# Identity attention's keys turned by transposes, their mean added behind them

## The reference

```
def _L0_tok_ref(x, W_h, b_h, W_o, b_o, W_r, b_r):     # patches of 16 samples and a mask
    hid = silu(einsum('bnd,dm->bnm', xm, W_h) + b_h)
    return einsum('bnm,mh->bnh', hid, W_o) + b_o + einsum('bnd,dh->bnh', xm, W_r) + b_r

def _L0_attn_ref(x):                                  # 16 heads of 16 columns
    xh = x.reshape(B, T, H, hd)
    x_centered = xh - mean(xh, axis=1)                # mean over the tokens
    corr = einsum('bthd,bThd->bhtT', x_centered, x_centered)
    return einsum('bhtT,bThd->bthd', softmax(corr, -1), xh)

h = _L0_tok_ref(x, ...)
h = h + _L0_attn_ref(_layernorm(h))
h = h + _L0_ffn_ref(_layernorm(h), ...)               # two layers, untouched here
```

## Time and profile before

| | us |
|---|---|
| median of 3 runs | 2703.74 |
| lowest and highest | 2702.42, 2705.84 |
| the profiled execution | 2703.38 |
| its span in the trace | 2701.6 |
| TensorE busy | 2600.9 (96% of the span) |
| VectorE busy | 1913.5 (71%) |
| ScalarE busy | 1702.6 (63%) |
| GpSimd busy | 1429.9 (53%) |

### The profile page before, as it was taken

The page is one execution under the profiler, slowest core; times in us unless marked ns, Lnnn a source line. Parts: engine busy times, 40 slices in busy tenths (PEclk is TensorE's granted clock), DMA queues, the critical chain, the costliest instruction groups (busy, mean ns, idle before and its releaser), DMA issues.

```text
span 2701.6 us, 71253 instructions
## 1 busy us (share of the span) xinstructions
PE 2600.9 (96%) x25088; PEld 2229.4 (83%) x25088; DVE 1913.5 (71%) x3771; ACT 1702.6 (63%) x4184; POOL 1429.9 (53%) x1520
## 2 busy tenths in 40 slices
PE   6999999969999999998999998999999998999998
PEld 4888888858888888877888887888888887888887
DVE  5777777658878788776656556887878877666664
ACT  3666666547778777774444435777777777444442
POOL 7888888557777776662000005777777665000000
PEclk9999999989999999998999999999999999999999
DMA  1111111111111111112111111111111111222221
GB/s 42 38 48 36 46 36 36 41 38 43 50 37 51 41 38 38 41 63 65 51 59 50 56 38 39 42 51 37 50 41 38 38 41 55 71 75 73 80 73 47
DMA packets 165614, 130.35 MB, mean 48 GB/s; under 512 B 23238, under 2 KB 163688, under 8 KB 165461
## 3 DMA queue, kind: packets, MB, share of 16 engines
q1 hardware_dynamic: 163157, 119.80, 14.3%
q0 software_dynamic: 2304, 8.47, 1.0%
HBM read 77.47 MB, written 50.33 MB: 47 GB/s over the span
## 4 chain that ended last, share of the span: by engine, by line
PE 48%; DVE 21%; ACT 20%; issue 7%; SPq 2%; DMA 1%; DVEq 1%; POOL 0%; ACTq 0%; POOLq 0%
ACT attn_E L1040 14%; PE const_banks L1317 6%; PE const_banks L1318 6%; PE const_banks L1319 6%; DVE attn_neg_top L1213 6%; DVE attn_ss L1206 5%; DVE attn_rot_b L1190 5%; ACT attn_sq L1077 5%; PE const_banks L1453 3%; PE const_banks L1452 3%; PE const_banks L1451 3%; PE const_banks L508 3%; PE const_banks L493 3%; PE const_banks L581 2%; PE const_banks L494 2%
## 5 line engine op out<-in xcount | busy, mean ns | idle before, releaser
L1040 ACT ACTIVATE attn_E<-const_banks,attn_nbias,attn_rn 128x128 f32<-128x128 f32 x1024 | 452.8, 462 | 144.9 <-DVE attn_nbias L1218 144.9
L977 POOL TENSOR_TENSOR attn_qk<-attn_rot_a,attn_rot_b 128x1024 f32<-128x1024 f32 x128 | 303.6, 2372 | 361.6 <-issue 296.2
L964 POOL TENSOR_TENSOR ffn_rstd<-ffn_var,const_neg_half 128x4 f32<-128x4 f32 x32 | 32.3, 1009 | 687.0 <-DVE ffn_var L1143 687.0
L1328 PE MATMUL const_banks<-weights_w_hi,attn_xT_hi 128*128 128x512 f32 x768 | 316.6, 412 | 1.2 <-DVE attn_oT_lo L1225 1.0
L1329 PE MATMUL const_banks<-weights_w_lo,attn_xT_hi 128*128 128x512 f32 x768 | 305.0, 397 | 0.0
L1330 PE MATMUL const_banks<-weights_w_hi,attn_xT_lo 128*128 128x512 f32 x768 | 304.8, 397 | 0.0
L1243 DVE SCALAR_TENSOR_TENSOR ffn_gated<-const_banks,weights_b_col,ffn_gate 128x512 f32<-128x512 f32 (+1 forms) x192 | 143.7, 749 | 216.3 <-ACT ffn_gate L1111 209.3
L1317 PE MATMUL const_banks<-ffn_xT_hi,ffn_w_hi 128*128 128x512 f32 x704 | 282.8, 402 | 6.9 <-DVE ffn_xT_lo L1155 5.4
L1318 PE MATMUL const_banks<-ffn_xT_lo,ffn_w_hi 128*128 128x512 f32 x704 | 279.5, 397 | 0.0
L1319 PE MATMUL const_banks<-ffn_xT_hi,ffn_w_lo 128*128 128x512 f32 x704 | 278.9, 396 | 0.0
L1111 ACT ACTIVATE ffn_gate<-const_banks,weights_b_col 128x512 f32<-128x512 f32 x160 | 110.1, 688 | 226.3 <-PE const_banks L1319 222.3
(11 more groups left out here) (178 smaller groups left out, 8009.9 us busy)
## 6 DMA issues: line engine op xcount, KB each, us to landing
attn_x_res<-xa SPq DMA_DIRECT2D x128, 128.0 KB, 4.9
xb<-attn_x_new SPq DMA_DIRECT2D x128, 128.0 KB, 1.7
ffn_x_<-xb SPq DMA_DIRECT2D x32, 512.0 KB
h<-ident_h SPq DMA_DIRECT2D x64, 128.0 KB, 1.7
xa<-ident_n SPq DMA_DIRECT2D x64, 128.0 KB, 1.7
attn_x_<-xa SPq DMA_DIRECT2D x128, 64.0 KB
xa<-ffn_x_new SPq DMA_DIRECT2D x16, 512.0 KB, 3.6
ffn_add<-h SPq DMA_DIRECT2D x16, 512.0 KB, 6.4
```

The costliest lines, as they stand in the source:

```text
L977: pool.tensor_tensor(qk[:, slot].rearrange("p a n -> p (a n)"), rot_a[:].rearrange("p a h d -> p (a h d)"), rot_b[:].rearrange("p a h d -> ...
L1040: last = act.activation(E[:, r, i], ps_s[:, r, i * P:(i + 1) * P], ACT.Exp, bias=nbias[:, r, i:i + 1], scale=rn[:, slot, h:h + 1], accum_o ...
L1328: pe.matmul(out_, xT_hi[:, slot, k], w.w_hi[:, k, cols], start=(k == 0), stop=False)
```

## The change

`centre` goes. The four matmuls of the keys become four transposes with the identity `c["ident"]`. VectorE sums the turned keys over the tokens, with the sign turned, into `nsum` (a new reduction between the two max reductions, which waits for the transposes). ScalarE's copy becomes four activations, one for each piece, that compute 128 v - sum, which is 128 times the centred value. The scores are then 128 x 128 times as large, and the exponential gets the scale 1/128^2. `cT_ready` is now counted up by the last of the four. On ScalarE the copy of the patches moves ahead of the keys' copy. GpSimd's preparation loses a memset and a select, and the counts of `cleared` and `pads` go down by one.

```diff
@@ front, GpSimd @@
-            for ap, value in ((centre[:], -1.0 / TOKENS), (sel[:], 0.0), (c["ident_b"][:], 0.0),
+            for ap, value in ((sel[:], 0.0), (c["ident_b"][:], 0.0),
                               (c["causal"][:], 0.0), (c["neg_half"][:], -0.5)):
                 pool.memset(ap, value).then_inc(cleared, 1)
-            pool.wait_ge(cleared, 6)
-            pool.affine_select(out=centre[:], in_=centre[:], compare_op=ALU.not_equal, fill=1.0 - 1.0 / TOKENS,
-                               base=0, pattern=[[-1, P]], channel_multiplier=1).then_inc(pads, 1)
+            pool.wait_ge(cleared, 5)
@@ ScalarE @@
-                if on(CENT):
-
-                    b = t - CENT
-                    need(act, s["cT_ps"], b + 1)
-                    need(act, s["S_ps"], b - 1)
-                    act.activation(cT[:, (u - CENT) % 2], ps_turn, ACT.Copy).then_inc(s["cT_ready"], 1)
                 if on(0) and u % 4 == 3:
...
                     act.activation(xT[:, u // 4], ps_hid[0:STACK], ACT.Copy).then_inc(xT_ready, 1)
+                if on(CENT):
+
+                    b = t - CENT
+                    need(act, s["summed"], b + 1)
+                    need(act, s["S_ps"], b - 1)
+                    for j in range(4):
+                        last = act.activation(cT[:, (u - CENT) % 2, j], ps_turn[:, j], ACT.Identity,
+                                              bias=nsum[:, (u - CENT) % 2, j:j + 1], scale=float(TOKENS))
+                    last.then_inc(s["cT_ready"], 1)
...
-                        act.activation(E[:, (u - SCORE) % 2, 2 * g:2 * g + 2], ps_S[:, 2 * g:2 * g + 2], ACT.Exp
-                                       ).then_inc(s["exp_done"], 1)
+                        act.activation(E[:, (u - SCORE) % 2, 2 * g:2 * g + 2], ps_S[:, 2 * g:2 * g + 2], ACT.Exp,
+                                       scale=1.0 / TOKENS ** 2).then_inc(s["exp_done"], 1)
@@ VectorE, between the max reductions of g = 0 and g = 1 @@
+                    if on(CENT) and g == 0:
+
+                        b = t - CENT
+                        need(dve, s["cT_ps"], b + 1)
+                        need(dve, s["cT_ready"], b - 1)
+                        dve.tensor_reduce(nsum[:, (u - CENT) % 2], ps_turn, AX_X, ALU.add, negate=True
+                                          ).then_inc(s["summed"], 1)
@@ TensorE @@
-                        last = pe.matmul(ps_turn[:, j], v1[:, slot, 4 * j:4 * j + 4].rearrange("p h d -> p (h d)"),
-                                         centre[:], start=True, stop=True)
+                        last = pe.transpose(ps_turn[:, j], v1[:, slot, 4 * j:4 * j + 4].rearrange("p h d -> p (h d)"),
+                                            c["ident"][:])
```

More of the change, by code:

```diff
@@ L145, in front @@
         v1 = n.sb("v1", [P, 4, IH, W])
-        centre = n.sb("centre", [P, P])
+        nsum = n.sb("nsum", [P, 2, 4])
         sel = n.sb("sel", [P, 4, P], BF16)
@@ L189, in front @@
         s = {k: n.sem(k) for k in (
-            "stat", "aggr", "eps", "rstd", "norm", "cT_ps", "cT_ready", "S_ps", "max_done", "mT_ps", "mT_ready",
+            "stat", "aggr", "eps", "rstd", "norm", "cT_ps", "summed", "cT_ready", "S_ps", "max_done", "mT_ps", "mT_ready",
             "shifted", "exp_done", "outT_ps", "outT_ready", "out_ps", "recip", "att_done", "h2_done", "stat2",
@@ L263, in front_pool @@
             pool.wait_ge(wo_split, 2)
-            pool.wait_ge(pads, 5)
+            pool.wait_ge(pads, 4)
             def cast(t, i, u, half):
@@ L397, in body @@
                     split(dve, wo_hi[:], wo_lo[:], wo_half[:], wo_split, 0)
-                    dve.wait_ge(pads, 5)
+                    dve.wait_ge(pads, 4)
                 if isinstance(t, int) and t == 9:
@@ L402, in body @@
                     silu(t - 1, 1)
-                if on(SCORE):
-                    b = t - SCORE
-                    for g in range(2):
+                for g in range(2):
+                    if on(SCORE):
+                        b = t - SCORE
                         need(dve, s["S_ps"], b + 1)
@@ L523, in body @@
                     if isinstance(t, int) and b == 0:
-                        pe.wait_ge(pads, 5)
+                        pe.wait_ge(pads, 4)
                         pe.wait_ge(sel_made, 4)
```

## The result

The changed kernel takes 2715.85 us (median, 2714.11 to 2716.72), the kernel before 2705.12 us (2702.42 to 2706.62) beside it. The ratio is 1.004 with a 95% interval of 1.0027 to 1.0053: slower by 10.7 us. The forecast was 7.6 us slower. The profiled execution of the changed kernel has a span of 2714.6 us, against 2701.6 before; 10 of these 13 us arise in the row loop of the front stage and its drain.

The account below looks back on a forecast made before the run. TensorE was taken to bound the front stage, its gain spent waiting on VectorE and ScalarE. Terms 1.8 - 4.1 + 7.2 + 2.7 gave +7.6 us, forecast 2711 us, range 2701 to 2723.

Parts of the forecast that it names:

- steps with the patches: Row-loop steps that turn four patches: the maxima's turn goes at +3.30, 0.29 us gained each, -4.1 us over 14 steps.
- with the casts: Steps with VectorE's x casts: the added sum delays the second hidden product, 0.55 us each, +7.2 us over 13 steps.
- the ordinary term: Ordinary row-loop steps: TensorE's whole 0.44 us gain is spent waiting; +0.06 us each, +1.8 us over 30 steps.
- The transposes: TensorE, keys' turn: four transposes replace eight matmul instructions, freeing 0.44 us per step, 28 us if TensorE never waited.
- The sum: VectorE, between the two max reductions: takes 0.69 us, from +1.27 to +1.96, and pushes the second max by 0.61.
- The pieces: ScalarE's keys' copy as four activations with a pointer: 0.37 us each, 1.18 for four, from +2.00 to +3.18.
- The rival at L1040's pace: ScalarE's four pieces at 0.36 us pitch, 1.54 for four: 26 us slower, 2730 us; chance 0.06.
- The new wait at L562: TensorE arrives at the maxima's turn at +2.71, waits for second max (+3.14) and fourth copy (+3.22); the 0.44 us is spent.
- The drain and its end: Front stage's last steps, t = 68 to 73: four at 0.29 us, then 0.7 and 0.8, together +2.7 us.
- The clock rival: TensorE's new gaps lower its clock; three steps at the low level add about 14 us, 2725 us; chance 0.03.

Follow-up runs that it names:

- e11: e9 with ScalarE's second normalisation moved from ahead of the patches' and keys' copies to behind the copy of the turned maxima; 2695.49 us, ratio 0.9963.
- e6: The changed kernel with three row_out matmuls moved ahead of L562 on TensorE and the first tanh ahead of the maxima's copy on ScalarE; 2716.71 us, ratio 1.0043.
- e9: e6 plus VectorE's first silu early and normalisation last, and only three output-product matmuls instead of six between maxima's turn and subtraction; 2705.52 us, ratio 1.0006.
- e3: The changed kernel with VectorE's three casts of the next patches moved behind silu(t, 0) and the normalisation; 2723.65 us, ratio 1.0064.

## Why the prediction was right, and where it was off

Right in direction and mechanism: slower, 10.7 us measured against 7.6 forecast, inside the range. The terms did not all come out, and their errors partly cancel: the 13 steps with the patches in the table gained some 1.5 us less than forecast, those with the casts cost some 1.4 less, and the loop's turn (1.4 where 0.4 was forecast among the ordinary steps) and the end of the drain (0.9) came on top. There are 31 steps left over for the ordinary term and not 30, which changes it by 0.06 us. The kinds of steps, from the starts of the transposes in both traces (t = 13 to 73):

| steps | forecast, each | before, mean | after, mean | sum of the change |
|---|---|---|---|---|
| ordinary, 22 steps | +0.06 | 7.73 | 7.79 | +1.5 |
| t % 8 = 0, 7 steps | +0.06 | 7.79 | 7.99 | +1.4 |
| with the patches, 13 steps | -0.29 | 8.16 | 7.99 | -2.2 |
| with the casts, 13 steps | +0.55 | 7.78 | 8.23 | +5.8 |
| t = 68 to 71 | +0.29 | 7.49 | 7.78 | +1.1 |
| t = 72 and 73 | +0.75 | 8.08 | 9.30 | +2.4 |

- **The transposes**: four instructions in 0.60 us, 0.44 freed. Right.
- **The sum**: 681 ns, from +1.27 to +1.95 without a wait. Forecast 0.69 and +1.96.
- **The pieces**: 366 ns each, four in 1.14. Forecast 0.37 and 1.18. The rival at L1040's pace fell. The estimate by the Trainium skill ("ScalarE: Activation LUTs", What ACT_TABLE_LOAD costs) was 1.27, and the trace is 0.13 below it.
- **The new wait at L562**: at +3.22, 0.35 us ahead of it in the row shown; the gain of TensorE is spent there. Right, and the transposes alone (0.9927) and the sum with a single copy (1.0008) show it.
- **Steps with the patches**: the mechanism was right, the size was not. I took the patches' copy at L547's end as in the earlier trace rows; ScalarE starts it 0.2 us behind that end. The pieces follow it at +2.24, L562 stands at +3.4 to +3.5 instead of +3.30:

```profile
336.07 0.66 PE L525 MATMUL const_banks<-const_ident,ident_outT 128*128 128x128 f32 x4
...
337.81 0.59 ACT L346 ACTIVATE tok_xT<-const_banks 84x512 fp32r<-84x512 f32 x1 [0.37 <-PE const_banks L495]
338.31 1.12 ACT L353 ACTIVATE ident_cT<-const_banks,ident_nsum 128x128 f32<-128x128 f32 x4
```

- **Steps with the casts**: +0.45 instead of +0.55. L445 takes 327 ns in the mean where L437 took 449 (both over 70 to 450 us), and every one of these casts ends 0.05 us behind the end of GpSimd's residual (L285, now L283), which reaches less far into it than before. That the long L437 of the earlier trace rows was a wait for GpSimd, and not the cast's own time, I had not seen; in e11, where the residual is over before the cast or at most 0.14 us into it, the same cast takes 185 ns. With the residual ending earlier, the second hidden product (L484) comes at +5.69 instead of the forecast +5.87.
- **The turn of the loop**, which I had not counted: every eighth step VectorE's first max starts at +0.21 instead of +0.13 and the pieces at +2.15 instead of +1.99. Before, L554's room of 0.66 us covered the most of it, and such a step took 0.07 more than an ordinary one; in the changed kernel it takes 0.24 more. Six of the seven steps grow by 0.23, the last (t = 64) by 0.04, 1.4 us together.
- **The drain and its end**: t = 68 to 71 as forecast. At t = 72 and 73 +2.4 instead of +1.5. L562 of t = 73 waits 2.00 us:

```profile
546.18 0.22 PE L562 MATMUL const_banks<-const_ident_b,ident_top 128*128 128x128 bf16 x1 [2.00 <-DVE ident_top L410]
...
550.48 2.09 PE L516 MATMUL const_banks<-ident_cT 32*128 32x128 f32 x32
```

  L516 takes 2.09 us here where it takes 1.17 in the loop: TensorE is at the low one of its two levels, 1.2 instead of 2.4 GHz (the granted clock of 550 to 555 us is 0.61), behind stretches in which it stood idle for 2 us. That is not new as such: the kernel before falls to that level too, and its L508 of t = 72, at 531.62, takes the same 2.09. But at t = 73 it takes only 1.31:

```profile
540.86 1.31 PE L508 MATMUL const_banks<-ident_cT 32*128 32x128 f32 x32
```

  So 0.78 us more stand in this one group of matmuls. How much of the +0.9 is the clock as a whole and how much the longer chain was not separated.
- **The clock rival** fell for the row loop: the granted clock is 1.00 with waits of 0.35 us in nearly every step and eight transposes among TensorE's work. The rule of the Trainium skill cited for it ("TensorE: Matmul & The Clock Gate", Part 4: PE-mode transpose), that transposes count for less, changes nothing here: 1.00 in each of the four stretches of 100 us. One reading against that rival was wrong: the gaps of the kernel before in 500 to 550 us are not of several us, the longest that TensorE waits there is 1.90 (ahead of L554 at 544.66).
- **What I missed as a whole** was the loop. I read L562 as a place where TensorE waits for two engines. It is a link of a chain that begins and ends at the scores. That gives nearly the same sum for the change, but a wrong forecast for e6, which filled the wait and gained nothing.

Of the rest of the 13 us between the profiled executions, 0.4 lie ahead of t = 13 and some 2.6 behind the start of t = 74, 0.9 of them in t = 74 and 75 and the others in the passage to the layers and in the layers, whose code is unchanged. Their cause stays open, and the medians show 10.7.

## What to carry to other kernels

Taking work off the busiest engine pays only as far as the loop through the other engines is shorter than that engine's work; add up that loop (here scores, maxima, sum, keys' copy, turn, subtraction, exponentials) before adding anything to it. When a wait has appeared, filling it moves it; what shortens the step is to take out of the loop the instructions that no dependence puts there, one after the other, as here three matmuls and one normalisation. And the same change cost 0.4% in the order that it came in, while in e9's order the kernel that has it is 0.3% faster than the one that has not (1.0006 against 1.0038), so judge a change again after reordering. The -0.4% of e11 is change and order together.

## What the runs showed of the hardware

- A float32 transpose of 128x128 is one matmul instruction, a float32 matmul with the same operands two: 0.60 against 1.06 us for four transposed tiles.
- A VectorE cast of 128x64 float32 in SBUF takes 0.18 us alone and 1.27 us when it starts inside a GpSimd tensor_tensor of 1.27 to 1.31 us (e3). VectorE's normalisation takes 0.67 us in e3 (L446), where a GpSimd cast is running when it starts, and 0.41 in the kernel before (L448), where it starts ahead of that cast.
- A sum over 512 float32 columns of PSUM takes 681 ns, a maximum over 1024 takes 1220 ns.
- An activation of 128 columns with one pointer takes 366 ns, without one 277 ns; one starts 0.26 us behind the other, since four take 1.14.
- In the changed kernel the turn of the loop delays VectorE's first max by 0.08 us and makes the step 0.24 longer than an ordinary one; in the kernel before 0.07.
